# Ten upsampled maps in place of sixteen, and a resize with the outer taps on edge rows alone

## Time and profile before

| What | Value |
|---|---|
| Median of 3 runs | 14506.09 us |
| Lowest and highest | 14485.17 and 14514.5 us |
| The profiled execution | 14479.08 us |
| Its span | 14477.3 us |
| Busy share PE, PEld, DVE, ACT, POOL | 78%, 60%, 60%, 66%, 48% |
| Granted TensorE clock, mean | 0.896 of full speed |
| Setup, to the load of the first image of x | 436.5 us |

### The profile page before, as it was taken

One profiled execution on the slowest core, in us unless ns is written; L12 is line 12 of the kernel. 1 busy time (PEld: TensorE's weight loads), 2 busy tenths in 40 slices (PEclk: granted clock), 3 DMA queues, 4 the chain that ended last, 5 costly groups with the idle time before them and its releaser, 6 DMA issues.

```text
span 14477.3 us, 470729 instructions
## 1 busy us (share of the span) xinstructions
PE 11349.7 (78%) x170988; PEld 8705.5 (60%) x170988; DVE 8630.8 (60%) x12547; ACT 9600.7 (66%) x20318; POOL 6951.3 (48%) x6167
## 2 busy tenths in 40 slices
PE   3568888888888888888888888888888888851887
PEld 2346666666666666666666666666666666641666
DVE  7436657566665756656665666566575666631743
ACT  1227777767777776777777777777777677751777
POOL 0005454545545454544545454454545454466467
PEclk9668999999999989999999999999899999975998
DMA  4214444444444444444444444444444444431444
GB/s 140 67 46 113 108 116 108 114 107 110 112 111 111 106 114 107 113 109 112 111 105 114 110 113 108 114 111 109 113 109 114 108 112 109 112 84 23 106 122 112
DMA packets 1848281, 1535.26 MB, mean 106 GB/s; under 512 B 1006880, under 2 KB 1382176, under 8 KB 1841760
## 3 DMA queue, kind: packets, MB, share of 16 engines
q1 hardware_dynamic: 1835776, 1494.30, 41.0%
q0 software_dynamic: 9216, 2.38, 0.2%
HBM read 1297.70 MB, written 198.21 MB: 103 GB/s over the span
## 4 chain that ended last, share of the span: by engine, by line
PE 36%; issue 15%; ACT 14%; ACTq 8%; DVE 7%; POOLq 6%; SPq 5%; DVEq 4%; POOL 4%; DMA 2%
ACTq L1166 6%; PE bank_small L926 6%; PE bank_small L977 5%; PE bank_scores L848 5%; PE windows L956 5%; PE bank_scores L865 4%; POOLq L635 3%; ACT hats L1165 3%; POOLq L637 2%; DVEq L1417 2%; POOL gbuf L706 2%; ACT pr L1117 2%; ACT hats L1167 2%; PE bank_turned L969 1%; PE bank_post L895 1%
## 5 line engine op out<-in xcount | busy, mean ns | idle before, releaser
L1473 DVE TENSOR_TENSOR prod<-windows,wy 128x640 f32<-128x640 f32 x4032 | 3278.2, 819 | 2680.0 <-PE windows L956 2640.0
L634 POOL TENSOR_TENSOR prod<-prod 128x768 f32<-128x768 f32 x1344 | 2462.6, 1832 | 2711.6 <-DVE prod L1473 2704.1
L956 PEld LDWEIGHTS windows<-fx,hats 64*64 64x64 f32 x129024 | 2721.5, 143 | 1367.7 <-issue 1298.2
L956 PE MATMUL windows<-fx,hats 64*64 64x80 f32 x129024 | 3341.0, 247 | 114.5 <-issue 105.3
L1165 ACT ACTIVATE hats<-hats,cst 128x512 f32<-128x512 f32 x4032 | 2877.8, 714 | 120.1 <-DMA hats<-sample_columns 84.3
L1418 DVE SCALAR_TENSOR_TENSOR ol<-xpad,lepw,ol 128x448 f32<-128x448 f32 x2688 | 2594.9, 965 | 236.0 <-issue 1.8
L1167 ACT ACTIVATE hats<-hats 128x512 f32<-128x512 f32 x4032 | 2541.7, 630 | 282.2 <-issue 10.4
L636 POOL TENSOR_TENSOR prod<-prod 128x384 f32<-128x384 f32 x1344 | 1580.6, 1176 | 212.3 <-issue 24.1
L926 PE MATMUL bank_small<-wom,ofp 128*128 128x216 f32 x8064 | 1627.9, 357 | 46.5 <-issue 46.5
L639 POOL TENSOR_TENSOR val<-prod 128x384 f32<-128x384 f32 x1344 | 1537.7, 1144 | 241.2 <-issue 159.9
L926 PEld LDWEIGHTS bank_small<-wom,ofp 128*128 128x128 f32 x8064 | 1470.5, 193 | 96.8 <-issue 52.7
(11 more groups left out here) (191 smaller groups left out, 13545.3 us busy)
## 6 DMA issues: line engine op xcount, KB each, us to landing
hats<-sample_columns SPq DMA_DIRECT2D x2688, 336.0 KB
ksel<-k_windows SPq DMA_DIRECT2D x3136, 32.0 KB
vsel<-v_windows SPq DMA_DIRECT2D x3136, 32.0 KB
fx<-map_columns SPq DMA_DIRECT2D x64, 420.0 KB
xpad<-in_x SPq DMA_DIRECT2D x17, 1568.0 KB, 14.1
map_columns<-fst SPq DMA_DIRECT2D x16, 1624.0 KB
feat_up<-fdense SPq DMA_DIRECT2D x16, 1568.0 KB, 14.1
q_windows<-qb SPq DMA_DIRECT2D x112, 224.0 KB, 2.7
```

Of the source, the lines that this page charges most:

```text
L634: pool.tensor_tensor(v[:, :, 0:n], v[:, :, 0:n], v[:, :, n:2 * n], ALU.add)
L956: last[h] = pe.matmul(o[m], hat[:, m], fx[XP * h:XP * h + XP, g, row:row + WR, :].rearrange("p r c -> p (r c)"), start=True, stop=True)
L1473: dve.tensor_tensor(o, x, w.unsqueeze(3).to_broadcast([128, 2, CP * WR, CG]), ALU.mult).then_inc(s_wm, 1)
```

## The change

The batch weights are computed once as `WBAT`. `MAP_OF[n]` numbers the distinct pairs, so that images 0 to 3 have map 0, images 4 to 11 maps 1 to 8 and images 12 to 15 map 9; `NMAP` is 10 and `FIRST[m]` is the first image of map m. Both DRAM tensors hold ten maps, the setup's loops on DVE, PE, ACT and SP run over ten, and the gathers' base `ibase` goes by `MAP_OF`. SP's loop over images is split by where the map advances with the image: i from 2 to 3 (map 0), 4 to 12 (map i - 3) and 13 to 15 (map 9); the body is written out in each. The other engines keep one loop. In the resize, taps 1 and 2 are one multiplication each over the full tile, with one addition, and taps 0 and 3 are computed and added for one row or column in seven each. The diff, without its unchanged lines:

```diff
@@ -84,9 +84,6 @@
-NCONST = const_layout()
@@ -94,6 +91,16 @@
+WBAT = resize_matrix(2, B).T
+MAP_OF = [0] * B
+for _n in range(1, B):
+    MAP_OF[_n] = MAP_OF[_n - 1] + int(not np.array_equal(WBAT[_n], WBAT[_n - 1]))
+NMAP = MAP_OF[NIMG - 1] + 1
+FIRST = [MAP_OF.index(m) for m in range(NMAP)]
+NCONST = const_layout()
@@ -115,7 +122,7 @@
-    put("ibase", (np.arange(B) * MROWS)[None])
+    put("ibase", (np.array(MAP_OF) * MROWS)[None])
@@ -129,15 +136,14 @@
-    mb = resize_matrix(2, B)
-    put("wbat", mb.T.reshape(1, -1))
+    put("wbat", WBAT.reshape(1, -1))
...
-    fmap = nc.dram_tensor("map_columns", (NIMG * MROWS, CG), F32, kind="Internal").ap()
+    fmap = nc.dram_tensor("map_columns", (NMAP * MROWS, CG), F32, kind="Internal").ap()
...
-    fup = nc.dram_tensor("feat_up", (NIMG, C, PIX), F32, kind="Internal").ap()
+    fup = nc.dram_tensor("feat_up", (NMAP, C, PIX), F32, kind="Internal").ap()
@@ -414,7 +420,7 @@
-                             fst[0][0:NIMG].rearrange("p g r c -> p (g r c)")).then_inc(s_tz, 16)
+                             fst[0][0:NMAP].rearrange("p g r c -> p (g r c)")).then_inc(s_tz, 16)
@@ -424,11 +430,11 @@
-            for i in range(NIMG):
+            for i in range(NMAP):
...
-                sp.wait_ge(s_fup[s], 16 * ((NIMG + 1 - s) // 2))
-                sp.wait_ge(s_tst[s], 16 * ((NIMG + 1 - s) // 2))
+                sp.wait_ge(s_fup[s], 16 * ((NMAP + 1 - s) // 2))
+                sp.wait_ge(s_tst[s], 16 * ((NMAP + 1 - s) // 2))
@@ -488,15 +494,22 @@
-            def feat_up_band(i, b):
+            def map_of(i, shift):
+                if isinstance(i, int):
+                    return MAP_OF[i]
+                return image(after(i, shift)) if isinstance(shift, int) else shift[0]
+            def feat_up_band(i, b, shift):
...
-                sp.dma_start(ub[b % 2], fup[bass.ds(image(i), 1), :, b * BAND:(b + 1) * BAND].rearrange(
+                sp.dma_start(ub[b % 2], fup[bass.ds(map_of(i, shift), 1), :, b * BAND:(b + 1) * BAND].rearrange(
...
-            def x_slot(i, n):
+            def x_slot(i, n, shift):
@@ -526,15 +539,15 @@
-                        feat_up_band(i, b)
-            def map_piece(i, p, done):
+                        feat_up_band(i, b, shift)
+            def map_piece(i, p, done, shift):
...
-                                 fm5[bass.ds(image(i), 1), 1:1 + W, :, r0 - 2:r1 - 2, :].rearrange(
+                                 fm5[bass.ds(map_of(i, shift), 1), 1:1 + W, :, r0 - 2:r1 - 2, :].rearrange(
@@ -567,7 +580,7 @@
-            def body(xi, di):
+            def body(xi, di, shift=None):
@@ -575,7 +588,7 @@
-                                    map_piece(di, 3, cnt(di, 2 * Q * NT, 0))
+                                    map_piece(di, 3, cnt(di, 2 * Q * NT, 0), shift)
@@ -584,8 +597,8 @@
-                                map_piece(xi, p, 0 if di is None else cnt(di, 2 * Q * NT, 2 * Q * t))
-                            x_slot(xi, n)
+                                map_piece(xi, p, 0 if di is None else cnt(di, 2 * Q * NT, 2 * Q * t), shift)
+                            x_slot(xi, n, shift)
@@ -597,8 +610,16 @@
-            with sp.Fori(2, NIMG) as i:
-                body((i, 0), (i, -1))
+            lo = 2
+            while lo < NIMG:
+                same = MAP_OF[lo] == MAP_OF[lo - 1]
+                hi = lo + 1
+                while hi < NIMG and (MAP_OF[hi] == MAP_OF[hi - 1]) == same:
+                    hi += 1
+                with sp.Fori(lo, hi) as i:
+                    body((i, 0), (i, -1), [MAP_OF[lo]] if same else MAP_OF[lo] - lo)
+                lo = hi
@@ -771,7 +792,7 @@
-            for n in range(NIMG):
+            for n in range(NMAP):
@@ -1274,29 +1295,52 @@
+            wv = wres.rearrange("p (t q r) -> p t q r", t=4, r=7)
...
-                for t in range(4):
-                    for q in range(8):
-                        wt = wres[:, t * H + 7 * q:t * H + 7 * q + 7].unsqueeze(2).to_broadcast([128, 7, SW])
-                        o = (rows_s[:, 7 * q:7 * q + 7, 1:1 + SW] if t == 0 else
-                             prod_s[:, q * 7 * SW:(q + 1) * 7 * SW].rearrange("p (r c) -> p r c", c=SW))
-                        dve.tensor_tensor(o, src[:, 8 * q + t:8 * q + t + 7, :], wt, ALU.mult)
-                    dve.drain()
-                    if t:
-                        o = rows_s[:, :, 1:1 + SW]
-                        dve.tensor_tensor(o, o, prod_s[:].rearrange("p (r c) -> p r c", c=SW), ALU.add)
-                        dve.drain()
-                pv = prod_s[:, 0:PIX].rearrange("p (r c) -> p r c", c=W)
-                for t in range(4):
-                    for q in range(8):
-                        wt = wres[:, t * H + 7 * q:t * H + 7 * q + 7].unsqueeze(1).to_broadcast([128, H, 7])
-                        o = (up_s[s][:] if t == 0 else pv)[:, :, 7 * q:7 * q + 7]
-                        dve.tensor_tensor(o, rows_s[:, :, 8 * q + t:8 * q + t + 7], wt, ALU.mult)
-                    dve.drain()
-                    if t:
-                        dve.tensor_tensor(up_s[s][:], up_s[s][:], pv, ALU.add)
-                        dve.drain()
+                ro = rows_s[:, :, 1:1 + SW]
+                pr_s = prod_s[:].rearrange("p (r c) -> p r c", c=SW)
+                def sevens(v):
+                    return v.rearrange("p (q r) c -> p q r c", r=7)
+                for t in (1, 2):
+                    x = src[:, t:t + SH, :].rearrange("p (q r) c -> p q r c", r=8)[:, :, 0:7, :]
+                    dve.tensor_tensor(sevens(ro if t == 1 else pr_s), x,
+                                      wv[:, t].unsqueeze(3).to_broadcast([128, 8, 7, SW]), ALU.mult)
+                dve.drain()
+                dve.tensor_tensor(ro, ro, pr_s, ALU.add)
+                dve.drain()
+                for t, r in ((0, 0), (3, 6)):
+                    r0, k = (0, 0) if t == 0 else (2, 7)
+                    x = src[:, r0:r0 + SH, :].rearrange("p (q r) c -> p q r c", r=8)[:, :, k, :]
+                    dve.tensor_tensor(pr_s[:, 8 * r:8 * r + 8, :], x, wv[:, t, :, r].unsqueeze(2).to_broadcast([128, 8, SW]),
+                                      ALU.mult)
+                dve.drain()
+                for r in (0, 6):
+                    o = sevens(ro)[:, :, r, :]
+                    dve.tensor_tensor(o, o, pr_s[:, 8 * r:8 * r + 8, :], ALU.add)
+                dve.drain()
+                up = up_s[s][:]
+                pu = prod_s[:, 0:PIX].rearrange("p (r c) -> p r c", c=W)
+                for t in (1, 2):
+                    x = rows_s[:, :, t:t + SW].rearrange("p y (q r) -> p y q r", r=8)[:, :, :, 0:7]
+                    dve.tensor_tensor((up if t == 1 else pu).rearrange("p y (q r) -> p y q r", r=7), x,
+                                      wv[:, t].unsqueeze(1).to_broadcast([128, H, 8, 7]), ALU.mult)
+                dve.drain()
+                dve.tensor_tensor(up, up, pu, ALU.add)
+                dve.drain()
+                pe_ = prod_s[:, 0:2 * H * 8].rearrange("p (k y q) -> p k y q", k=2, y=H)
+                for n, (t, r) in enumerate(((0, 0), (3, 6))):
+                    x = rows_s[:, :, (0, 2)[n]:(0, 2)[n] + SW].rearrange("p y (q r) -> p y q r", r=8)[:, :, :, (0, 7)[n]]
+                    dve.tensor_tensor(pe_[:, n], x, wv[:, t, :, r].unsqueeze(1).to_broadcast([128, H, 8]), ALU.mult)
+                dve.drain()
+                for n, r in enumerate((0, 6)):
+                    o = up.rearrange("p y (q r) -> p y q r", r=7)[:, :, :, r]
+                    dve.tensor_tensor(o, o, pe_[:, n], ALU.add)
+                dve.drain()
@@ -1306,9 +1350,9 @@
-                dve.tensor_scalar(f, u[0], wbat[:, 2 * n:2 * n + 1], None, ALU.mult)
-                dve.drain()
-                dve.scalar_tensor_tensor(out=f, in0=u[1], scalar=wbat[:, 2 * n + 1:2 * n + 2], in1=f,
+                dve.tensor_scalar(f, u[0], wbat[:, 2 * FIRST[n]:2 * FIRST[n] + 1], None, ALU.mult)
+                dve.drain()
+                dve.scalar_tensor_tensor(out=f, in0=u[1], scalar=wbat[:, 2 * FIRST[n] + 1:2 * FIRST[n] + 2], in1=f,
@@ -1321,14 +1365,14 @@
-            for n in range(NIMG):
-                if n + 1 < NIMG:
+            for n in range(NMAP):
+                if n + 1 < NMAP:
...
-                dve.wait_ge(s_fup[s], 16 * ((NIMG + 1 - s) // 2))
-                dve.wait_ge(s_tst[s], 16 * ((NIMG + 1 - s) // 2))
+                dve.wait_ge(s_fup[s], 16 * ((NMAP + 1 - s) // 2))
+                dve.wait_ge(s_tst[s], 16 * ((NMAP + 1 - s) // 2))
```

## The result

The changed kernel takes 14235.5 us (median of four runs, 14225.5 to 14246.0), beside 14501.4 for the kernel before: ratio 0.9817, interval 0.9800 to 0.9834. It is faster by 266 us where 150 were forecast, outside the range. On another chip later the same kernel gave 0.9832 (0.9819 to 0.9846). The profiled execution took 14234.65 us, 244.4 less than that of before.

A forecast was written before the change was run, and what follows sets the result against it. It took TensorE as busy nearly throughout the main part, with a 436 us setup ahead that nothing overlaps. Resize 57.6 plus maps 92.7 gave 150.3 us off 14506.1, so 14355.8 us, with eight in ten between 14328 and 14386.

The forecast's parts named there:

- The resize: Setup, DVE: two small maps' resize falls from 112.6 to 55.0 us, saving 57.6 us, low end 48.8.
- The rival of slow strides: Resize on DVE: small strided column instructions run slower, at most 8.8 us more, 14364.6; chance 0.12.
- The maps: Setup, DVE and PE: six map periods fewer at 15.46 us each save 92.7 us, bounds 89 to 97.
- The setup's other parts: Setup: border stores stay hidden with 49 us to spare, weight loads move forward, fills vary 2 us either way.
- The main part ... I take 0: Loop over images: same DMAs, SP's two jumps fewer change nothing, 0 us; bounds 10 us gained or lost.
- the step on the fills: Setup: DVE's issue gaps between fills may fall elsewhere, with 166 instructions less before them; 2 us either way.
- as long as the main part is left alone: Condition: nothing of the main part overlaps the 436 us setup, so whatever the setup loses comes off the end.
- The jump: SP's loop: a jump back costs SP about 5 us, hidden under PE's work; eleven jumps in place of thirteen.
- the clock of the first pass: Rival, first pass of attention: TensorE's granted clock shifts by a tenth, 42 us, 14314 or 14398; chance 0.05 for both.
- further tile took the general path: Rival, main part: changed last bits send one more tile to the gathers, 405.8 us more, 14762; chance 0.01.
- NMAP was 10: Rival, setup: clamped images' weights differ in a bit, NMAP is 16, only the resize saves, 14448; 0.01 or less.

The follow-up runs named there:

- b_pe90: The kernel before with 90 empty waits added on PE in the setup and nothing else changed: 14358.1 us beside 14485.4, ratio 0.9915.
- a_pe166: The changed kernel with 166 empty waits added on PE alone in the setup: ratio 0.9889 to the kernel before.

## Why the prediction was wrong

- **The resize**: 112.6 - 57.3 (23.43 to 80.70) = 55.3 us saved, forecast 57.6. The full-tile instructions came at 3.89 and 3.42, as worked out, and the 512-element ones at 0.65 for 0.62. The row pass was given five drains and has four, which is 0.1 us. The strided ones of 448 were put at 0.55 and took 0.91 to 0.93 each (two in 1.82 and 1.85), 1.9 ns an element in place of 1.05: eight of them cost 2.9 us more than forecast, which covers the missing 2.3. The rival of slow strides was right in kind, inside its bound of 3.5 ns. The Trainium skill's penalty for each new 16-byte line (SBUF — State Buffer, "Door 1: The DMA port swizzle") agrees with this row, at a stride of 28 and 32 bytes.
- **The maps**: the first `fdense` to the load of x was 299.6 us and is 207.3, so 92.4 us for six maps, forecast 92.7. The period is (211.3 - 86.0) / 8 = 15.7, where 15.46 was read before.
- **The setup's other parts** held: border stores and fills cost nothing that shows.
- **"The main part ... I take 0"** is the step that failed, with its bounds of 10 us. It looked at SP's jumps and at what the main part computes; three loops on SP brought nothing that shows, as b_pe90, with one, has the shorter main part (13255.0 against 13293.2). It did not ask where the other engines' loops lie once their setup is shorter, although the count of instructions removed stood in the step on the fills, for DVE alone. The condition "as long as the main part is left alone" was taken as met because no line of it was edited. The runs put 62 to 104 us on PE's position alone in one direction (a_pe166) and 127 in the other (b_pe90).
- **The jump** was priced on SP only. Its own rows carried the clue, 5 us on SP's queue behind a jump, and it did not read the same stop on PE. The rule quoted from the Trainium skill (Runtime: NRT & Kernel Launch, "Instruction fetch mechanics") covers the stop at the jump, and the trace agrees (3.4 to 3.9 us on PE at the thirteen jumps before). The second stop, at the next block's edge when little of the first block is left, that rule does not state; the traces show it, and I had not asked whether the next block would be there in time.
- **The other rivals** missed: the clock of the first pass did not move (0.64 and 422.8 us), no further tile took the general path (the gathers' iteration is there once), and NMAP was 10.

**Why a first block of 75 instructions cost 9 us an iteration and not 4.** Twelve iterations took 9973.9 us before and 9860.8 in b_pe90, 113.1 less:

```profile
2732.40:12706.30 9973.90, 8288.83 (x127560) 6389.03 (x127560) 6289.68 (x9181) 7138.83 (x15145) 5010.25 (x4369) 0.92 0.44 111
```

```profile
2714.80:12575.60 9860.80, 8239.55 (x127560) 6357.35 (x127560) 6265.24 (x9181) 7139.61 (x15145) 5011.73 (x4368) 0.93 0.45 112
```

The second stops are 43.9 us of it. Another 49.3 are TensorE's own busy time, for the same 127,560 matmuls. In the 15 us behind the same jump the granted clock is 0.66 with the second stop and 0.85 without (a window of before, then of b_pe90; over the first nine jumps such windows show 0.66 to 0.77 before and 0.77 to 0.85 in b_pe90):

```profile
6896.70:6911.70 15.00, 7.23 (x62) 6.33 (x66) 1.95 (x4) 3.10 (x5) 4.95 (x5) 0.66 0.56 118
```

```profile
6817.30:6832.30 15.00, 9.63 (x168) 8.29 (x172) 6.93 (x10) 7.76 (x17) 5.64 (x6) 0.85 0.66 161
```

Over the twelve iterations the trace's record of the clock has TensorE at the lower of its two levels (1.2 GHz in place of 2.4) for 1508.7 us before and for 1385.8 in b_pe90. So with the second stops TensorE runs its matmuls at the lower level for longer; that the stops are the reason is read from the place of the windows and was not separated by a run. The remaining 20 us were not settled, nor was the first to last difference of 38 us between b_pe90 and the changed kernel, which have the same place on PE and other places on DVE, ACT and SP.

## What to carry to other kernels

Removing or adding instructions ahead of a long hardware loop moves the loop's head within its fetch block; here that was worth 0.85% with nothing else changed. So compare two versions of such a kernel only after looking for an "issue" wait a fixed number of instructions behind the branch, and count the instructions of every engine, modulo 256 on PE, before calling an untouched loop unchanged. Place the head so that the first block holds a few microseconds of work (here 141 instructions cost nothing that could be told, and 75 did).

## What was not expected of the hardware

- PE's second fetch stall (1 to 6 us at the thirteen jumps of the kernel before), and that it all but goes between 75 and 141 instructions left.
- Ninety idle instructions made the kernel 127 us faster.
- Removing 3 to 8 us stops from ACT, DVE and POOL at every image boundary gained nothing while PE still stood there.
- DVE took 1.9 ns an element at strides of 28 and 32 bytes, and 1.05 ns in runs of seven.
